# A 96-byte statistics buffer declared behind all other SBUF tiles instead of in their middle

## What is computed

```python
def reference(x, Wqkv, Wout, W1, b1, W2, b2):
    xn = layernorm(x)                          # eps 1e-5, no scale or shift
    # attention: 16 heads of 16, segments of 512 tokens,
    # keys and values: every 8th token of the segment (64 of them)
    q, k, v = split(xn @ Wqkv.T); q = q * 16 ** -0.5
    scores = q @ k.T                           # per segment and head
    c = max of scores over each block of 64 queries, per key
    w = exp(scores - c)
    att = (w @ v) / (sum(w) + 1e-10)
    # feed-forward: 256 -> 1024 -> 256
    ffn = relu(xn @ W1 + b1) @ W2 + b2
    return x + att @ Wout.T + ffn
```

## Time and profile before

| | |
|---|---|
| timed, median of 3 | 1087.45 us (1087.24 to 1091.53) |
| profiled execution | 1083.8 us, its span 1082.0 us |
| TensorE busy | 1062.5 us, 98% |
| VectorE busy | 818.5 us, 76% |
| ScalarE busy | 648.6 us, 60% |
| GpSimd busy | 622.9 us, 58% |
| DMA moved | 216.38 MB, mean 200 GB/s |
| instructions | 19173 |

### The profile page before, as it was taken

One profiled execution on the slowest core, in us unless ns is written; L12 is line 12 of the kernel. 1 busy time (PEld: TensorE's weight loads), 2 busy tenths in 40 slices (PEclk: granted clock), 3 DMA queues, 4 the chain that ended last, 5 costly groups with the idle time before them and its releaser, 6 DMA issues.

```text
span 1082.0 us, 19173 instructions
## 1 busy us (share of the span) xinstructions
PE 1062.5 (98%) x5381; PEld 811.8 (75%) x5381; DVE 818.5 (76%) x1465; ACT 648.6 (60%) x1080; POOL 622.9 (58%) x487
## 2 busy tenths in 40 slices
PE   6999999999999999999999999999999999999998
PEld 4577778777787777787777777777877777777777
DVE  8877787777777876877767778778778778787753
ACT  5656665656655566665656656566555665656663
POOL 5355565655565656555656656555565565556565
PEclk9999999999999999999999999999999999999999
DMA  5457777676876777776777776768767677767644
GB/s 189 111 151 214 222 214 209 182 221 195 237 215 190 195 205 222 214 216 199 198 208 223 217 206 176 230 191 238 215 187 202 199 227 210 213 166 219 190 143 142
DMA packets 153576, 216.38 MB, mean 200 GB/s; under 512 B 27344, under 2 KB 96720, under 8 KB 153552
## 3 DMA queue, kind: packets, MB, share of 16 engines
q1 hardware_dynamic: 153408, 215.96, 69.3%
q10 hardware_dynamic: 144, 0.13, 0.0%
HBM read 100.41 MB, written 58.46 MB: 147 GB/s over the span
## 4 chain that ended last, share of the span: by engine, by line
PE 93%; DMA 2%; DVE 2%; SPq 1%; issue 1%; ACT 0%; POOL 0%; DVEq 0%; POOLq 0%
PE h_bank L1023 40%; PE y_bank L1023 39%; PE s_banks L1096 5%; PE misc L1203 3%; PE s_banks L1203 2%; PE misc L1023 2%; DMA w_exp<-w 1%; DVE xn L824 1%; DVE s_max L841 1%; DMA k_dram<-k_lo 0%; DMA yt_dram<-y_mem 0%; DVE w_exp L847 0%; SPq L406 0%; PE misc L1169 0%; PE misc L1141 0%
## 5 line engine op out<-in xcount | busy, mean ns | idle before, releaser
L533 POOL TENSOR_TENSOR h_lo<-h_full,h_hi 128x512 fp32r<-128x512 f32 x256 | 336.9, 1317 | 392.5 <-ACT h_full L614 389.1
L620 ACT ACTIVATE w_exp<-w_exp 128x512 f32<-128x512 f32 x256 | 161.6, 632 | 241.8 <-DVE w_exp L847 240.0
L612 ACT ACTIVATE h_hi<-h_bank,b_cols 128x512 fp32r<-128x512 f32 x256 | 174.8, 683 | 78.2 <-PE h_bank L1023 72.0
L1023 PE MATMUL h_bank<-xt_hi,w_hi 128*128 128x512 f32 x512 | 208.8, 408 | 0.0
L1023 PE MATMUL h_bank<-xt_hi,w_lo 128*128 128x512 f32 x512 | 202.3, 395 | 0.0
L1023 PE MATMUL h_bank<-xt_lo,w_hi 128*128 128x512 f32 x512 | 201.8, 394 | 0.0
L841 DVE TENSOR_REDUCE s_max<-s_banks 128x8 f32<-128x512 f32 x254 | 171.1, 674 | 39.7 <-PE s_banks L1096 39.7
L1023 PE MATMUL y_bank<-h_hi,w_hi 128*128 128x512 f32 x496 | 197.0, 397 | 0.1
L1023 PE MATMUL y_bank<-h_hi,w_lo 128*128 128x512 f32 x496 | 196.3, 396 | 0.0
L1023 PE MATMUL y_bank<-h_lo,w_hi 128*128 128x512 f32 x496 | 195.7, 395 | 0.0
L847 DVE TENSOR_TENSOR w_exp<-s_banks,s_max 128x512 f32<-128x512 f32 x254 | 175.6, 691 | 11.0
(11 more groups left out here) (139 smaller groups left out, 1513.9 us busy)
## 6 DMA issues: line engine op xcount, KB each, us to landing
q_pack<-q_hi SPq DMA_DIRECT2D x248, 128.0 KB, 2.4
rden_rows<-rden_dram SPq DMA_DIRECT2D x128, 128.0 KB, 4.6
x_b<-x SPq DMA_DIRECT2D x32, 512.0 KB, 4.4
x_raw<-x SPq DMA_DIRECT2D x31, 512.0 KB, 4.9
q_pack<-q_lo SPq DMA_DIRECT2D x124, 128.0 KB, 2.4
yt_dram<-y_mem SPq DMA_DIRECT2D x124, 128.0 KB, 3.6
y_mem<-yt_dram SPq DMA_DIRECT2D x31, 512.0 KB, 4.4
out<-x_b SPq DMA_DIRECT2D x31, 512.0 KB, 3.1
```

The lines of the kernel that those rows point to most:

```text
L533: pool.tensor_tensor(h_part[1][:, i % HBUF], h_full[:, i % HBUF], f32(h_part[0][:, i % HBUF]), ALU.subtract).then_inc(h_lo, 1)
L612: act.activation(h_part[0][:, i % HBUF], h_bank[i % 2][:], ACT.Relu, bias=b1_cols[:, i:i + 1]).then_inc(h_hi, 1)
L620: act.activation(w_exp[:, pair], w_exp[:, pair], ACT.Exp).then_inc(w_ready, 1)
L1023: mm = pe.matmul(ps, stationary[a], moving[b], start=start and c == 0 and n == 0, stop=stop and c == len(pairs) - 1 and n == 2, skip_group ...
```

## The change

The declaration of `stats_second` moves from behind `stats` to behind `y_mem`, the last tile. Its 96 bytes per partition leave the middle, so that each tile from `mean_var` to `y_mem` starts 96 bytes lower, and `stats_second` itself takes the 96 bytes behind `y_mem`. The tiles declared ahead of it (identity, masks, weights, `x_raw`, `x_keys`, `x_b2`, `stats`) stay. No instruction, wait or transfer changes otherwise.

```diff
         stats = sb("stats", [P, T + 1, 6], F32)
-        stats_second = sb("stats_second", [P, T, 6], F32)
         mean_var = sb("mean_var", [P, T + 1, 2], F32)
...
         y_mem = sb("y_mem", [P, 2, T * D], F32)
+        stats_second = sb("stats_second", [P, T, 6], F32)
         y_blocks = y_mem[:, 0].rearrange("p (i a t n) -> p i a t n", i=P // PW, a=DH, t=T)
```

## The result

The changed kernel takes 1070.95 us (median of 4; 1069.53 to 1072.79) against 1087.35 us for the kernel before in the same comparison (1084.37 to 1091.53). The ratio is 0.9847, with an interval of 0.9811 to 0.9884: it is faster by 1.5%. The forecast, 1087.4 us with a range of 1083.5 to 1091.8, missed it. The profiled execution took 1070.42 us, its span 1068.6.

The account below looks back on a forecast made before the run. TensorE's matmul pace was taken to bound the body. Terms for TensorE, other engines, transfers and start, each 0, summed to 0 us, so the timed median was forecast at 1087.4 us, range 1083.5 to 1091.8.

Parts of the forecast that it names:

- The bound: Kernel body, 100 to 1000 us: how fast matmuls follow one another on TensorE sets the time; busy 898.11 of 900 us.
- TensorE, put at zero: Matmuls and weight loads: new tile starts change nothing, 0 us, bounds -8.2 to +14.6 us.
- the one place with equal starts: `xt` streaming while `k_pack` loads, both at 64, ahead of a score product: pitch 0.23 us, so equal starts do no harm.
- the bound below: TensorE's largest gain, from the fastest pitch read, 0.2317 against 0.2335 us: 0.8% of 1062.5 us, -8.2 us.
- Rival (c): TensorE faster: slow pitches are the present residues' fault, all go to 0.2317; -8.2 us, 1079.2 us; 5%.
- Rival (b): TensorE slower: weights and moving operands at one residue disturb each other; +14.6 us, 1102 us; 3%.
- (d): No effect because tiles do not come to lie as declared; same time, 1087.4 us; 2%.
- Rival (a): Transfers slower: reads at 224 delay `k_pack`, the score product stalls in each of 31 steps; 37 us, 1124 us; 5%.
- Other engines, put at zero: ScalarE, VectorE and GpSimd: off the path in the body, idle time covers any change; 0 us, bounded by 6.7 us.
- Transfers, put at zero with up to 1 us for the thin steps: DMA loads and stores: 1.8 us of cover hides changes; 0 us, 0.5 to 1 us bound where steps have less cover.
- The start, put at zero with 1.2 us as bound: Opening weight load, 11.01 us of the chain, with `w_exp` going from 64 to 224: 0 us; at 11%, 1.2 us.
- The range: Whole kernel: 1083.5 to 1091.8 us, from executions seen plus 0.3 us margin, holding 87%; rivals (a), (b), (c) left out.

Follow-up runs that it names:

- the padding kernels: Kernel before or changed kernel with unused floats ahead of `b2_rows` or `mean_var`; ahead of `b2_rows`, ratio 0.9985 on the kernel before, 0.9851 on the changed one.
- the second profile of the changed kernel: Changed kernel run again as it is, with more executions, against the kernel before: 1070.16 us, ratio 0.9850.
- the kernel with all tiles at 0: Changed kernel with 32 unused bytes ahead of `b2_rows`, large tiles at multiples of 256: 1068.55 us, ratio 0.9851; run again, 1066.68 us, 0.9818.
- distance 64: Changed kernel with 16 unused floats ahead of `mean_var`, so the later tiles start 32 past a multiple of 256 and the weights stay at 224.
- `xt_lo` aside: Changed kernel with `stats_second` between `xt_hi` and `xt_lo` and 160 unused bytes behind `xt_lo`, which alone starts at 64: 1076.53 us, ratio 0.9911.
- the last two kernels: Changed kernel run again as it is, 1070.16 us, and with 32 unused bytes ahead of `b2_rows`, 1066.68 us; both on one chip.

## Why the prediction was wrong

**The bound.** Right: TensorE's pace sets the time of the body, and the whole gain is in it.

**TensorE, put at zero.** This is the step that failed; measured, it is -15.7 us of busy time. Three things went wrong in it. First, the comparison. The argument set `xt` at 64 against `wkv` at 224 and found equal groups (395 and 394 ns), as though the start of the moving operand were the cause. But the weight of the `wkv` product is `xkey`, which is at 64, so both products had distances off zero, 96 and 160. Equal means showed that both were slow. After the change they are both at 390. Second, the one place with equal starts. It was read only for harm: 0.23 us from 501.57 to 501.80 is "no slower". Over all repetitions these intervals ahead of the score products are 230.0 to 231.0 ns before, at eleven of the twelve places inside the two steps, in a pattern with a mean of 233.3; at three of them the pattern's 237 or 238 was due. They were a sign of a gain in the trace, though not of its size, since they stand among disturbed ones. Third, the bound below. -8.2 us came from the fastest of the three runs read (0.2317), but all 128-row matmuls of that kernel were disturbed, and the undisturbed pace, 0.2267, isn't in its trace: no six in a row are under 0.2308. With 0.2267 in place of 0.2317 the same sum would give -31 us; the measured -15.7 lies between, since score products and what follows them keep a slower pace.

**Rival (c).** It named the direction and the mechanism, slow pitches as the fault of the present residues, and got 5% and 8.2 us; the time came out 8 us below its 1079.2. "The durations agree", held against it, was the comparison that could not speak. Rival (b), the same pair with the other sign, is refuted: equal starts are the quick case. Of (d), the starts did move as declared, since the pace follows them in the padding kernels. Rival (a) asked for a wait in some thirty steps; there are five.

**Other engines, put at zero.** Right. `h_lo` takes 1314 ns against 1317, `x_b2` 2444 against 2450 (groups by form after):

```profile
L533 POOL TENSOR_TENSOR h_lo<-h_full,h_hi 128x512 fp32r<-128x512 f32 x256 | 336.1, 1314 | 382.2 <-ACT h_full L614 378.8 <-PE y_bank L1023 1.3
...
L553 POOL TENSOR_TENSOR x_b<-x_b,b_rows 128x1024 f32<-128x1024 f32 x32 | 78.2, 2444 | 0.0
```

**Transfers, put at zero with up to 1 us for the thin steps.** Right for nearly all steps, too small in sum. The issues after, as in the earlier trace rows (queue, count, KB each, median us to landing):

```profile
x_b<-x SPq DMA_DIRECT2D x32, 512.0 KB, 4.5
...
yt_dram<-y_mem SPq DMA_DIRECT2D x124, 128.0 KB, 3.6
y_mem<-yt_dram SPq DMA_DIRECT2D x31, 512.0 KB, 4.7
...
k_pack<-k_dram SPq DMA_DIRECT2D x93, 128.0 KB, 2.6
...
k_dram<-k_hi SPq DMA_DIRECT2D x31, 128.0 KB, 2.7
```

`y_mem` lands 0.3 us later, the store of the high keys 0.7 us earlier, that of the low keys 0.3 us later (3.5 against 3.2, and 3.9 in the second profile of the changed kernel), the others are where they were. The loads of `k_pack` wait for the low keys' store. The waits for `k_pack` are 3.5 and 5.0 us in two profiles where under 1 us was forecast. Two causes offer themselves: the matmuls that cover the transfers are over sooner, and the queue is busier, 72.5% against 69.3%. The first alone doesn't make the wait, since the kernel with all tiles at 0 has the quick pace too and waits 0.2 and 1.1 us at shares of 68.9% and 68.7%. The second isn't shown: over the other kernels the wait doesn't follow the share (3.3 us at 69.7% with distance 64, 1.1 us at 72.3% with `xt_lo` aside).

The rule of the Trainium skill (DMA: Bandwidth & Descriptors, How a descriptor splits into AXI transactions) gives reads off a 256-byte boundary more to fetch the further they start past it. The shares of this case agree in their ends: 68.0% to 68.9% with the moving tiles at 0, 71.0% at 192, 72.5% and 72.8% at 224; in the middle they are not in order (69.7% at 32, 69.0% at 128), and the store of `y_mem` did not grow by the 15% of a row's beats, which would have been 0.5 us by an estimate from that page: it is 3.6 us at 64 and at 224, and 3.4 to 3.5 with the tiles at 0. Whether the rule is the cause of the 3.5 us between the last two kernels is not shown; they go the other way from the change's result and are smaller than it.

**The start, put at zero with 1.2 us as bound.** Nothing here speaks against zero. Where the load of the weights stands in the chain again, in the second profile of the changed kernel, it takes 11.24 us against 11.01. The wait in the opening was 6.1 us before and 7.7 and 6.6 in two profiles after, but over all kernels it lay anywhere from 6.0 to 7.9 us, with 6.3 and 7.9 where the moving tiles are at 0, so it does not follow the start.

**The range.** It was built from the spread of the runs, and left out what the bounds of TensorE allowed. A term with bounds of -8.2 and +14.6 us and no row that tested equal starts was given 8% of the chances.

## What to carry to other kernels

Where TensorE is the bound and weights are loaded beside streaming matmuls, look at the starts of the tiles modulo 256 bytes as a pair, the moving operand and the weights loaded while it streams: here equal starts gave 2.2% on the pitch and 1.5% on the time, with no instruction changed. A small buffer in the middle of the declarations can undo that, so put odd-sized tiles last; whether multiples of 256 are better still than other equal starts the last two kernels make likely and don't settle. When a trace is used as its own control, check that the two groups differ in the disputed property and in nothing else that could be it: here it was a property of a pair, and both groups stood on the same side.

## What was unexpected of the hardware

The pace of a 128x128 by 128x512 matmul depends on the distance, in SBUF, between the start of its moving operand and that of the weights that are loaded while it streams (one odd load takes its interval from 226.8 to 236.7 ns and leaves the next ones slow): 226.7 ns at distance 0, a repeating 230.6, 231.6, 237.8 ns at 96, in part quick at 64, slow at 32 and at 128 to 224.

A disturbance lasts: the four intervals from a 96-row score product on stay 4 to 11 ns above 226.6, some 27 ns for each of 248, although `q_pack`, `k_pack` and the weights all lie at one residue. This is some 6.7 us that remain in the changed kernel. The same four intervals of about 236, 228, 232 and 231 ns stand behind the first matmul that follows the 64-row value products, so it isn't the 96 rows alone. What causes it was not tried and stays open, as does the in-between pace at distance 64.
